# Sixteen-head attention: q and k in two twelve-bit parts as float32r, scores in one matmul, in a two-layer kernel on one Trainium2 core

## The reference

```python
Q, K, V = (proj(W_Q), proj(W_K), proj(W_V))      # (B, 16, T, 16)
Q = _apply_rope(Q, cos, sin)
K = _apply_rope(K, cos, sin)
scores = einsum('bhsd,bhtd->bhst', Q, K) / sqrt(16)
scores = where(causal, scores, -inf)
attn = softmax(scores, axis=-1)
out = einsum('bhst,bhtd->bhsd', attn, V)
x = x + einsum('bsd,ed->bse', out, W_O)
```

## Time and profile before

| | |
|---|---|
| median of 3 runs | 2645.7 us |
| lowest and highest | 2637.13 and 2647.03 us |
| span of the profiled execution, first to last instruction | 2633.8 us |
| mean granted TensorE clock, share of full speed | 0.981 |
| instructions | 57555 |
| DMA | 159.33 MB in 225600 packets, mean 60 GB/s |

### The profile page before, as it was taken

One profiled execution on the slowest core, in us unless ns is written; L12 is line 12 of the kernel. 1 busy time (PEld: TensorE's weight loads), 2 busy tenths in 40 slices (PEclk: granted clock), 3 DMA queues, 4 the chain that ended last, 5 costly groups with the idle time before them and its releaser, 6 DMA issues.

```text
span 2633.8 us, 57555 instructions
## 1 busy us (share of the span) xinstructions
PE 2442.8 (93%) x21618; PEld 1121.3 (43%) x21618; DVE 1990.4 (76%) x4256; ACT 1552.1 (59%) x2785; POOL 597.8 (23%) x584
## 2 busy tenths in 40 slices
PE   6898799999999999999899999999999999999995
PEld 4544333434445353443444444353444533433344
DVE  4777888887858879687877787878686798788822
ACT  2335466665655656565555766656565566666761
POOL 5564210304133040311314112130313300000011
PEclk9999899999999999999999999999999999999997
DMA  2433220212213122130311313121131222111110
GB/s 54 115 83 93 85 82 20 73 49 62 69 34 87 55 82 57 50 90 21 86 49 49 101 50 90 26 74 55 41 83 34 72 62 61 39 48 40 30 43 26
DMA packets 225600, 159.33 MB, mean 60 GB/s; under 512 B 91824, under 2 KB 225072, under 8 KB 225328
## 3 DMA queue, kind: packets, MB, share of 16 engines
q1 hardware_dynamic: 224560, 154.75, 21.2%
q10 hardware_dynamic: 768, 0.92, 0.1%
HBM read 87.36 MB, written 67.63 MB: 59 GB/s over the span
## 4 chain that ended last, share of the span: by engine, by line
PE 65%; DVE 20%; ACT 5%; issue 4%; SPq 2%; POOL 2%; DMA 2%; DVEq 1%; POOLq 0%; ACTq 0%
PE psum L1777 14%; PE psum L1754 13%; DVE mx L1475 12%; PE psum L1725 7%; PE psum L1691 4%; ACT probs L1249 3%; PE psum L1655 2%; PE psum L1808 2%; PE psum L1565 2%; PE psum L1626 2%; PE psum L1828 2%; PE psum L1816 2%; PE psum L1797 2%; PE psum L1595 2%; PE psum L1712 2%
## 5 line engine op out<-in xcount | busy, mean ns | idle before, releaser
L1249 ACT ACTIVATE probs<-psum 128x512 f32<-128x512 f32 x2176 | 1142.5, 604 | 557.4 <-PE psum L1754 311.0
L1475 DVE TENSOR_REDUCE mx<-psum 128x1 f32<-128x512 f32 (+2 forms) x2304 | 1289.1, 620 | 239.7 <-PE psum L1725 183.7
L1754 PE MATMUL psum<-qst,kst 34*128 34x512 bf16 (+7 forms) x5120 | 659.5, 349 | 46.8 <-DVE mx L1475 15.7
L1777 PE MATMUL psum<-probs,vs 128*17 128x512 f32 (+3 forms) x5120 | 581.9, 536 | 0.7
L1725 PE MATMUL psum<-kst,qst 64*128 64x512 bf16 (+3 forms) x2560 | 427.5, 351 | 37.0 <-DVE mx L1475 16.2
L1754 PEld LDWEIGHTS psum<-qst,kst 64*128 64x128 bf16 (+1 forms) x5120 | 193.7, 94 | 393.5 <-ACT probs L1249 117.0
L1725 PEld LDWEIGHTS psum<-kst,qst 64*128 64x128 bf16 x2560 | 129.2, 93 | 348.4 <-ACT probs L1249 141.0
L1777 PEld LDWEIGHTS psum<-probs,vs 128*17 128x17 f32 x5120 | 93.0, 95 | 183.2 <-issue 153.3
L1043 POOL TENSOR_SCALAR vare<-mv 128x4 f32<-128x4 f32 x64 | 15.3, 239 | 562.4 <-DVE mv L1351 562.4
L1072 POOL TENSOR_TENSOR sums<-probs 128x512 f32<-128x512 f32 x12 | 15.3, 1272 | 529.4 <-ACT probs L1199 529.4
L1732 PE MATMUL psum<-maskq,identh 64*128 64x64 bf16 (+1 forms) x2048 | 126.9, 204 | 0.0
(11 more groups left out here) (160 smaller groups left out, 2839.7 us busy)
## 6 DMA issues: line engine op xcount, KB each, us to landing
qk_dram<-parts SPq DMA_DIRECT2D x224, 128.0 KB
qst<-qk_dram SPq DMA_DIRECT2D x384, 64.0 KB, 2.1
kst<-qk_dram SPq DMA_DIRECT2D x384, 64.0 KB, 2.0
v_dram<-vst SPq DMA_DIRECT2D x64, 136.0 KB, 3.9
vs<-v_dram SPq DMA_DIRECT2D x64, 136.0 KB, 2.1
xs<-x_in SPq DMA_DIRECT2D x16, 512.0 KB, 3.9
x_dram<-xs SPq DMA_DIRECT2D x16, 512.0 KB, 2.9
att_dram<-ast SPq DMA_DIRECT2D x64, 128.0 KB, 2.0
```

Source lines behind the costliest of these rows:

```text
L1249: act.activation(dst, src, ACT.Exp, scale=DK1 ** -0.5).then_inc(S["exp"], 1)
L1475: ins = dve.tensor_reduce(mx1[:, n % 2, 2 * g + odd, tile % TPC, c:c + 1], bank(src, at, at + cols), AX.X, ALU.max)
L1754: ins = pe.matmul(two[odd][:, at:at + cols], kst[rows, kslot, part, pair, keys], qst[rows, qslot, part, pair, CH - cols:CH], start=(part = ...
L1777: ins = pe.matmul(bank(7, off, CH, rows=VW, row=32 * h), vtile[:, h, :], probs[:, HG * (step_no(b, hg, k) % 2) + h, at:at + CH - off], sta ...
```

## The change

q and k are split into two parts, `hi` (rounded to float32r by ScalarE) and the difference, both stored as four-byte values. `mid` and `lo` and the tile `resid` go. Three pieces of each tile are stored (q: hi, hi, rest; k: hi, rest, hi), and a block of q or k is loaded with two transfers. A head then has 48 rows in SBUF, with the two rows of the maximum behind them 50. The max pass runs over the 48 rows and the scores over the 50 in one matmul per head, both as float32r; the mask matmuls stay bf16. The planner is told the new durations, and so writes a new order.

```diff
-PARTS = 3
-STORED = ((0, 1, 2, 0), (0, 1, 0, 2))
-PAIRED = ((0, 0), (0, 1))
+STORED = ((0, 0, 1), (0, 1, 0))
+PARTS = 2
+PROWS = len(STORED[0]) * DK1
...
-        add("DVE", "res", (*c, bl), key(0.3), 0.61, ("hi", (*c, bl)), ("lo", old), free=("RT", (*c, bl)))
-        add("ACT", "mid", (*c, bl), key(0.3), 0.53, ("res", (*c, bl)))
-        add("POOL", "lo", (*c, bl), key(0.3), 1.12, ("mid", (*c, bl)))
-        add("SP", "put", (*c, bl), key(0.3), 0.6, ("lo", (*c, bl)), lat=5.0)
+        add("DVE", "res", (*c, bl), key(0.3), 0.61, ("hi", (*c, bl)), free=("RT", (*c, bl)))
+        add("SP", "put", (*c, bl), key(0.9), 0.5, ("res", (*c, bl)), lat=4.0)
...
-        add("SP", "load k", me, pos - LEAD - 25, 0.4, ("put", (b, q, 2 * (hg // 2) + 1)),
+        add("SP", "load k", me, pos - LEAD - 25, 0.15, ("put", (b, q, 2 * (hg // 2) + 1)),
...
-                add("PE", "scores", (b, hg, k, j), key + j, 0.43 * size + (0.09 * len(pieces) if diagonal else 0),
+                add("PE", "scores", (b, hg, k, j), key + j, 0.215 * size + (0.09 * len(pieces) if diagonal else 0),
...
-        resid = sb("resid", [P, 2, CH], F32)
-        parts = sb("parts", [P, 2, PARTS, CH], BF16)
+        parts = sb("parts", [P, 2, PARTS, CH], F32)
...
-        kst = sb("kst", [P, KRING, 2, HG // 2, CH], BF16)
-        qst = sb("qst", [P, QRING, 2, HG // 2, CH], BF16)
+        kst = sb("kst", [P, KRING, HG // 2, CH], F32)
+        qst = sb("qst", [P, QRING, HG // 2, CH], F32)
...
-        nmaxT1 = sb("nmaxT1", [HG * MAXROWS * TPC, 2, P], BF16)
+        nmaxT1 = sb("nmaxT1", [HG * MAXROWS * TPC, 2, P], F32)
...
-                        for part, row, first in [(0, 0, PAIRED[side][0]), (0, REST, PAIRED[side][1]), (1, 0, 2)]:
-                            row += HALF * odd
-                            sp.dma_start(into[row:row + REST, slot, part, :, :],
-                                         of[first:first + 2, :, :, :].rearrange("n d g t -> (n d) g t")
-                                         ).then_inc(loaded, 16)
+                        sp.dma_start(into[HALF * odd:HALF * odd + PROWS, slot, :, :],
+                                     of.rearrange("n d g t -> (n d) g t")).then_inc(loaded, 16)
...
-                    act.activation(split(b, bl)[:, 0, :], home("RT", item), ACT.Copy).then_inc(S["hi"], 1)
-                elif kind == "mid":
...
+                    act.activation(split(b, bl)[:, 0, :].bitcast(F32R), home("RT", item), ACT.Copy).then_inc(S["hi"], 1)
...
-                    dve.tensor_tensor(resid[:, bl % 2, :], home("RT", item), split(b, bl)[:, 0, :], ALU.subtract
+                    dve.tensor_tensor(split(b, bl)[:, 1, :], home("RT", item), split(b, bl)[:, 0, :], ALU.subtract
...
-                            rows = slice(HALF * odd, HALF * (odd + 1))
+                            rows = slice(HALF * odd, HALF * odd + PROWS)
                             ins = pe.matmul(two[odd][:, at:at + cols],
-                                            qst[rows, qslot, 0, pair, P * (tile % TPC):P * (tile % TPC + 1)],
-                                            kst[rows, kslot, 0, pair, 0:cols], start=True, stop=c < q)
+                                            qst[rows, qslot, pair, P * (tile % TPC):P * (tile % TPC + 1)].bitcast(F32R),
+                                            kst[rows, kslot, pair, 0:cols].bitcast(F32R), start=True, stop=c < q)
...
-                        for part in range(2):
-                            for odd in range(2):
-                                rows = slice(HALF * odd, HALF * odd + (HALF if part == 0 else RROWS))
-                                ins = pe.matmul(two[odd][:, at:at + cols], kst[rows, kslot, part, pair, keys],
-                                                qst[rows, qslot, part, pair, CH - cols:CH],
-                                                start=(part == 0), stop=(part == 1 and not diagonal))
+                        for odd in range(2):
+                            rows = slice(HALF * odd, HALF * odd + PROWS + MAXROWS)
+                            ins = pe.matmul(two[odd][:, at:at + cols], kst[rows, kslot, pair, keys].bitcast(F32R),
+                                            qst[rows, qslot, pair, CH - cols:CH].bitcast(F32R),
+                                            start=True, stop=not diagonal)
```

More of the change, by code:

```diff
@@ L13 @@
 BF16 = mybir.dt.bfloat16
+F32R = mybir.dt.float32r
 FP8 = mybir.dt.float8e4
@@ L461, in chunk_jobs @@
     for bl in range(4):
-        n = 4 * chunk_no(b, q) + bl - 2
-        old = (*CHUNKS[n // 4], n % 4) if n >= 0 else None
         there = parts_before(b, q, bl)
@@ L484, in head_jobs @@
         slot = block_before(b, hg, q, KRING)
-        add("SP", "load k", me, pos - LEAD - 25, 0.4, ("put", (b, q, 2 * (hg // 2) + 1)),
+        add("SP", "load k", me, pos - LEAD - 25, 0.15, ("put", (b, q, 2 * (hg // 2) + 1)),
             *(scored_with(*slot) if slot else []), lat=4.5)
         slot = block_before(b, hg, q, QRING)
-        add("SP", "load q", me, pos - LEAD - 25, 0.4, ("put", (b, q, 2 * (hg // 2))),
+        add("SP", "load q", me, pos - LEAD - 25, 0.15, ("put", (b, q, 2 * (hg // 2))),
             *(scored_for(*slot) if slot else []), lat=4.5)
@@ L761, in build @@
         kact = attT
-        lent_parts = xp[:, :, :, :].rearrange("p s t d -> p (s t d)").bitcast(BF16)[:, 0:2 * PARTS * CH]
+        lent_parts = xp[:, :, :, :].rearrange("p s t d -> p (s t d)")
         lent_parts = lent_parts.rearrange("p (r n c) -> p r n c", r=2, n=PARTS)
@@ L775, in build @@
         att_dram = nc.dram_tensor("att_dram", [B, T, D], F32, kind="Internal").ap()
-        qk_dram = nc.dram_tensor("qk_dram", [B, 2, H, len(STORED[0]), DK1, T], BF16, kind="Internal").ap()
+        qk_dram = nc.dram_tensor("qk_dram", [B, 2, H, len(STORED[0]), DK1, T], F32, kind="Internal").ap()
         v_dram = nc.dram_tensor("v_dram", [B, NHG, P, NT, HG * VW], F32, kind="Internal").ap()
@@ L814, in k_loaded @@
             n = block_no(b, hg, c)
-            wt.wait_ge(f"load k {n % KRING}", 96 * (n // KRING + 1))
+            wt.wait_ge(f"load k {n % KRING}", 32 * (n // KRING + 1))
         def q_loaded(wt, b, hg, q):
             n = block_no(b, hg, q)
-            wt.wait_ge(f"load q {n % QRING}", 96 * (n // QRING + 1))
+            wt.wait_ge(f"load q {n % QRING}", 32 * (n // QRING + 1))
         def rows_written(wt, b, hg, q):
@@ L901, in _ @@
                     half, side = divmod(bl, 2)
-                    wt.job("lo", item)
+                    wt.job("res", item)
                     for n, part in enumerate(STORED[side]):
@@ L951, in _ @@
                     for odd in range(2):
-                        row = HALF * odd + REST
-                        sp.dma_start(qst[row:row + MAXROWS, n % QRING, 1, :, :],
+                        row = HALF * odd + PROWS
+                        sp.dma_start(qst[row:row + MAXROWS, n % QRING, :, :],
                                      nmaxT1[16 * odd:16 * (odd + 1), n % 2, :]).then_inc(S[f"rows {n % QRING}"], 16)
@@ L1048, in _ @@
                     elif pieces < KRING:
-                        pool.memset(kst[:, pieces, 1, :, :], 1.0).then_inc(done, 1)
+                        pool.memset(kst[:, pieces, :, :], 1.0).then_inc(done, 1)
                         pieces += 1
@@ L1099, in _ @@
                                        ).then_inc(S["roped"], 1)
-                elif kind == "lo":
-                    b, q, bl = item
-                    wt.job("res", item)
-                    wt.job("mid", item)
-                    pool.tensor_tensor(split(b, bl)[:, 2, :], resid[:, bl % 2, :], split(b, bl)[:, 1, :],
-                                       ALU.subtract).then_inc(S["lo"], 1)
                 elif kind == "carry":
```

6 lines of the change are left out of this document (removed).

## The result

The changed kernel takes **2766.9 us** in the median of four runs (2760.81 to 2772.13), against 2645.64 for the kernel before: a ratio of 1.048, with a 95% interval from 1.044 to 1.051. The prediction was 2500 us and faster. It missed the size and the sign.

The account below looks back on a forecast made before the run. TensorE was taken to bound the kernel, VectorE taking turns. Removed score matmuls -234 us, weight loads +28 and +32, give -174; VectorE returns 31, net -143: span 2491, median about 2500 us, range 2405 to 2605.

Parts of the forecast that it names:

- The price of a float32r pair: Max and score matmuls on TensorE: a float32r pair of 512 columns costs the bf16 price, 0.22 us.
- Rival (d): TensorE, both passes: two clocks per four-byte column, 234 us more on TensorE, about 2835 us; chance 0.07.
- The weight loads: TensorE: 0.07 us per float32r load, exposed at narrow pairs (28 us) and openings (32 us).
- rival (a): TensorE: slow weight loads at 0.11 us each, leaving -87 us on TensorE, 2566 us; chance 0.20.
- Stored and loaded long before use: Transfers of the parts: bytes written grow by half, yet lie beside TensorE and count as nothing in the sum.
- My sign for this case: Changed profile: pairs at 0.22 us with a gain under 100 us would put the error in VectorE and the banks.
- VectorE's cap: Stretches of 100 us: VectorE may fill at most 88.6%, which binds in nine and gives back 31 us.
- rival (b): VectorE and ScalarE take over early: VectorE held to 84% of a stretch, 88 us come back, 2560 us; chance 0.12.
- The clock: TensorE's granted clock: a lower level could take back up to 50 us; not in the sum, widens the upper side.

Follow-up runs that it names:

- the same order with fewer bytes: Changed kernel, order of every queue kept, each tile's parts stored in two pieces instead of three, four load transfers per block instead of two: 2704.97 us.
- the type alone: Changed kernel with max and score matmuls reading only the upper 16 bits of each value as bf16 instead of float32r, same order and transfers: 2667.66 us.
- two bf16 parts: Changed kernel's layout with q and k as two packed bf16 parts (16 bits instead of 24), store planned at 2.0 + 4.0 us: 2523.23 us.
- The store told: Changed kernel with the planner given 4.0 us of SyncE for a store of the parts instead of 0.5, landing kept at 4.0: 2658.27 us.

## Why the prediction was wrong

**The price of a float32r pair: right.** I took the bf16 price, 0.22 us, over the bounds of 0.43 and 0.86. In a stream it is 0.235 to 0.242 us. Rival (d), two clocks for each column, had the right sign for the wrong reason: its point of decision was a pair over 0.32 us, and only pairs at breaks come near or pass it (0.314 behind a mask, 0.336 to 0.338 after another layout). The Trainium skill, FP8 and Floating Point Precision, TensorE Precision Notes, gives true FP32 four passes and has the reduced form truncate what it reads. If the reduced form takes one pass, an estimate by that rule is a quarter of the 0.86 us, 0.215; the trace, with 0.235 to 0.242, lies 9 to 13% above it.

**The weight loads: the second largest error.** I took 0.07 us a load from the 141 ns transpose. The record is 186 ns, rival (a)'s. But the cost came by another way than rival (a)'s sum had it. I laid loads one behind another in a queue and let them hide behind columns. In the trace the loads of the two row halves start 3 to 4 ns apart (1404.397 and 1404.401 us, then 1404.506 and 1404.509) and last 182 to 187 ns, so they run side by side. At 1415.107 a pair's loads start 1 ns after the last mask pair has started, and its matmuls 28 ns later; there is little ahead for the loads to hide behind. That this is why the pair pays is my reading; that it pays is in the table: about 0.1 us wherever short masks or another layout stand ahead. I had charged only narrow pairs and openings, 60 us in all. Openings (717 pairs) and pairs behind masks (977) each pay it, the full-width ones too: 717 x 0.098 + 977 x 0.086 is 154 us by the medians of the table. Taking the type away took 150 us from TensorE's busy time and, after 63 us more of idle time, gave 99 us back. The rule that I set against my price (the Trainium skill, TensorE: Matmul & The Clock Gate, Weight-path perf modes: no fast load for FP32) was the right one: float32r loads as slowly as FP32 here.

**"Stored and loaded long before use": the largest error.** I costed the store at nothing, with a sentence, because the parts are *loaded* long after. What I did not ask is who waits for the *slot* that they leave. Before, `put` told the planner 0.6 and 5.0 us for four transfers of half the size, behind two more steps, `mid` on ScalarE and `lo` on GpSimd; the change says 0.5 and 4.0 for three of twice the size each, right behind `res`. The 8.46 us at 914.45 are that error. ScalarE's copy for the tile after next stands in an in-order queue ahead of the exponentials, and with it stand the banks and TensorE. I had read ScalarE as a beneficiary (64 copies less) and not as the engine that the store can stop. Told to the planner, the store gave back 109 us. My sign for this case pointed elsewhere: pairs near 0.22 us and a gain under 100 us were to mean an error in the step on VectorE and the banks.

**VectorE's cap: the mechanism is there, its size is not settled.** In the changed kernel VectorE holds 17% of the chain, less than the 20% before. Where the losses are gone it holds 28%, and halving its reduces gives 66 us. My sum had 31 and rival (b) 88, but for another quantity: what VectorE takes back of TensorE's gain, not all that half its reduces are worth. My rule let a stretch shrink until VectorE fills 88.6% of it; at an average of 77% VectorE already takes turns.

**The clock: no term, and it should have been one.** Half clock went from 101 to 303 us. If all of that extra time would have run at twice the rate, it is 101 us, the largest that it can be; my outer bound was 50. The runs of the changed layout that plan the store longer lie at 142 to 217, the same order with fewer bytes at 220, the one with the type alone at 320. So a large part of it goes with the waits at the store and not with the type. Nor does it go with TensorE's idle time as a whole: two bf16 parts have 249 us idle and 142 at half clock, the kernel before 181 and 101. What goes along is the time in long pauses, as in the stall above: pauses of TensorE of over 1 us add up to 84 us before, 154 in the changed kernel, 163 with the type alone, 108 with two pieces in the same order, and 80 to 106 where the store is planned longer. The store told has 88 us of them and still 200 at half clock, where the kernel before has 101; that rest stays open. How much of the loss of each edit is clock and how much the wait itself, the runs do not separate.

**The sum.** Predicted were -146 us and measured +121, 267 apart. Taking both losses out gave 202 of these: the kernel then takes 2565, 65 us above the prediction. Halving VectorE's reduces gives 66 more, 2499, but that this meets the forecast of 2500 is a coincidence: the forecast had 31 us for VectorE in it, and without them it would be 2469. So some 30 us are left even with the loads as cheap as bf16, the store planned longer and half of VectorE's reduces gone. The clock, with 159 us at half clock there against 101 before, and no term in the sum, can hold up to 29 of them; it is not shown that it does.

## What to carry to other kernels

An operation's price in a stream is not its price at a break: count how often it follows something short or of another kind, and give those places a price of their own. Where an order is planned from given durations, go through every duration that the change alters, the transfers above all, and ask who reuses each buffer and what stands behind the waiting instruction in its queue; here one planned number was worth as much as the choice of the number format. Before taking a wider format for its bits, try the narrow one in the same layout and weigh what it gives up.

## What was not expected of the hardware

- Weight loads of two row halves run side by side, in the median 3 ns apart over the changed kernel's 1280 pairs, and a float32r pair costs about 0.1 us more wherever short masks or matmuls of another layout stand ahead.
- float32r costs 0.235 us for 512 columns in two halves, with a load record of 182 to 186 ns; the float32 transpose, also four bytes, loads in 141 ns.
- A store of 256 KB usually holds SyncE for 0.64 us at issue, but up to 2.9 (lines of the changed kernel, ns min/median/max):

```profile
L902 SPq DMA_DIRECT2D qk_dram<-parts x168: 570/640/2947, 92.0 to 2231.2; - x168
```

- Stretches with a granted clock of 0.80 and 0.90 stood in a kernel whose TensorE is busy 90%. Two of them in the changed kernel, in the columns of the earlier trace rows:

```profile
300.00:400.00 100.00, 82.44 (x528) 38.41 (x528) 72.10 (x163) 38.91 (x72) 14.59 (x13) 0.80 0.26 78
900.00:1000.00 100.00, 86.75 (x793) 41.55 (x791) 74.97 (x155) 57.87 (x109) 4.84 (x7) 0.90 0.28 78
```

The first of them had 0.97 before. The second holds the stall of 8.8 us: the lower level was granted from 908.8 us on for 13.7 us, to 922.5 us, so the 6.8 us of work after the resumption at 915.7 ran at half rate.
